# Second cross attention in units of 6, 6 and 4 heads, with expert products taken in beside it

## The reference

```python
# L1_xattn_ref: 16 heads of 16, against 77 rows of context, with masks
att = einsum('bhsd,bhtd->bhst', q, k) / sqrt(d);  att = where(mask == 0, -1e9, att)
out = einsum('bhst,bhtd->bhsd', softmax(att), v);  x = x + out
# L1_ffn_ref, attention part: 8 experts, each row weighted by a gate
n1 = layernorm(x) * w + b;  rw = gating(n1, smha_sim, smha_gates)
q, k, v = (einsum('btc,ech,bte->bth', n1, proj, rw) for proj in (q_proj, k_proj, v_proj))
attn = softmax(causal(q @ k.T * scale)) @ v
hs = x + einsum('bth,ehc,bte->btc', attn, o_proj, rw)
```

## Time and profile before

| | us |
|---|---|
| median of 3 runs | 1319.3 (1313.14 to 1320.17) |
| profiled execution, its own time | 1325.34 |
| its span | 1323.6 |
| TensorE busy in the span | 1177.9 (89%) |
| VectorE busy | 851.8 (64%) |
| ScalarE busy | 555.9 (42%) |

### The profile page before, as it was taken

The page is one execution under the profiler, slowest core; times in us unless marked ns, Lnnn a source line. Parts: engine busy times, 40 slices in busy tenths (PEclk is TensorE's granted clock), DMA queues, the critical chain, the costliest instruction groups (busy, mean ns, idle before and its releaser), DMA issues. The chain is left out here.

```text
span 1323.6 us, 19885 instructions
## 1 busy us (share of the span) xinstructions
PE 1177.9 (89%) x7124; PEld 838.7 (63%) x7124; DVE 851.8 (64%) x1832; ACT 555.9 (42%) x1209; POOL 256.6 (19%) x426
## 2 busy tenths in 40 slices
PE   8788999898888889899889788999988787899998
PEld 4343333333333348677567677999967677789888
DVE  5577777877646668556568777756534355865555
ACT  6205666665656445455235453010032333543332
POOL 5012222222220037344102220000010112400000
PEclk9979999999979779999899998999989889999999
DMA  7840373330614510000030000000030000000000
GB/s 212 202 96 2 56 64 50 50 49 25 104 22 96 103 45 18 0 0 1 0 128 1 1 1 1 1 0 1 0 128 1 1 1 0 1 0 17 17 17 16
DMA packets 38000, 50.70 MB, mean 38 GB/s; under 512 B 11130, under 2 KB 28816, under 8 KB 37264
## 3 DMA queue, kind: packets, MB, share of 16 engines
q1 hardware_dynamic: 37904, 49.44, 17.6%
HBM read 37.26 MB, written 11.77 MB: 37 GB/s over the span
## 5 line engine op out<-in xcount | busy, mean ns | idle before, releaser
L577 PE MATMUL PS<-ARENA 128*17 128x512 f32 (+19 forms) x2208 | 395.2, 426 | 62.8 <-DVE ARENA L1752 14.8
L577 PEld LDWEIGHTS PS<-ARENA 128*17 128x17 f32 (+6 forms) x2208 | 159.4, 124 | 220.3 <-issue 123.6
L1352 ACT ACTIVATE ARENA<-PS 128x512 f32<-128x512 f32 (+3 forms) x384 | 169.8, 495 | 135.7 <-PE PS L577 133.4
L1752 DVE TENSOR_REDUCE ARENA<-PS 128x1 f32<-128x128 f32 (+7 forms) x256 | 182.9, 750 | 46.1 <-PE PS L577 44.3
L577 PE MATMUL PS<-WQKVP,TRR 128*128 128x384 f32 x512 | 134.1, 344 | 1.5 <-ACT BC L1279 1.0
L2184 POOL TENSOR_SCALAR_AFFINE_SELECT ARENA<-ARENA 128x128 f32<-128x128 f32 x256 | 74.3, 299 | 224.8 <-ACT ARENA L1352 222.9
L577 PEld LDWEIGHTS PS<-W2P,INT 128*128 128x128 f32 x768 | 95.1, 188 | 2.9
L577 PE MATMUL PS<-W2P,INT 128*128 128x256 f32 x768 | 95.5, 279 | 0.0
L577 PEld LDWEIGHTS PS<-WQKVP,TRR 128*128 128x128 f32 x512 | 93.4, 192 | 2.6 <-ACT BC L1279 1.9
L2030 DVE SCALAR_TENSOR_TENSOR ARENA<-PS,rw,ARENA 128x384 f32<-128x384 f32 x112 | 69.2, 617 | 39.2 <-PE PS L577 37.9
L577 PE MATMUL PS<-TRR,W1P 128*128 128x512 f32 x256 | 88.3, 406 | 5.8 <-ACT BC L1279 5.8
(11 more groups left out here) (224 smaller groups left out, 1926.5 us busy)
## 6 DMA issues: line engine op xcount, KB each, us to landing
ARENA<-qk_parts SPq DMA_DIRECT2D x96, 128.0 KB, 5.4
ARENA<-xq_parts SPq DMA_DIRECT2D x48, 128.0 KB, 5.7
qk_parts<-ARENA SPq DMA_DIRECT2D x6, 768.0 KB, 3.3
ARENA<-in_w SPq DMA_DIRECT2D x2, 2048.0 KB, 10.5
xq_parts<-ARENA SPq DMA_DIRECT2D x8, 384.0 KB, 2.6
ARENA<-in_wqkv SPq DMA_DIRECT2D x1, 3072.0 KB, 11.4
X<-in_x SPq DMA_DIRECT2D x4, 512.0 KB, 6.7
ARENA<-in_wf SPq DMA_DIRECT2D x2, 1024.0 KB, 8.9
```

What stands on the lines that cost most here:

```text
L577: return nc.tensor.matmul(o, lhsT, rhs, start=start, stop=stop, **kw)
L1352: ins = nc.scalar.activation(PROB[GRP * (step % 2) + j][:, 0:w], PS[:, uses[key][0], 0:w], ACT.Exp, scale=HD ** -0.5)
L1752: ins = v.tensor_reduce(negm[:, n % 2, TPB * j + st:TPB * j + st + 1], PS[:, bank:bank + 2, :].rearrange("p b s -> p (b s)")[:, 0:P * (st ...
```

## The change

The cross attention is cut into three units a tile, of 6, 6 and 4 heads (462, 462 and 308 columns), 48 in all. A unit's scores now fill one bank; the units take banks 0, 1 and 2 in turn. Transposes of one unit take one bank (3 or 4 in turn), with four, four and three pieces. Values are 4, 4 and 3 fp32 matmuls of 102, 102 and 68 columns, into bank 5 for every tile. `EX` and `PTS` slots are of 512 columns, and the columns beyond the heads are cleared once by GpSimd.

One list, `expert_plan()`, now sets the order of the cross attention and of the products on TensorE, VectorE, ScalarE and GpSimd. From step 23 on it puts products beside the units, three, three and two in three steps, so that 32 products (four tiles) stand in 12 steps: those of a chunk begin in the step in which its gate is done. Until the tenth tile they take banks 6 and 7 alone, then 6, 7, 0 and 1. The normalization and gate work of a chunk is cut into halves of two tiles and spread over steps 0 to 11 behind the chunk. Products of the last eight tiles but a few stand behind the last unit. The split of the expert weights goes every second step from the eighth on (before: every third from the fourth).

In the row attention, the transposes of `P1` stand ahead of those of `ATT`. Buffers move in SBUF.

```diff
+GATE_LAG, QUOTA, WEIGHTS_AT = 23, (3, 3, 2), 8
+def chunk_ops(c, at):
+    if at == 1:
+        yield "lean", c
+    if at in (2, 3):
+        yield "stat", c, at - 2
+    if at in (4, 5):
+        yield "center", c, at - 4
+    if at in (6, 7):
+        yield "scale", c, at - 6
+    if at in (7, 8):
+        yield "turn_n1", c, at - 7
+        yield "square", c, at - 7
+    if at in (8, 9):
+        yield "lower", c, at - 8
+    if at == 9:
+        yield "logits", c
+def expert_plan():
+    period = 4 * PER_TILE
...
+        while count > 0 and sent < len(products) and u >= period * (products[sent][0] // 4) + GATE_LAG:
+            i, e = products[sent]
+            yield "product", i, e
+            if i > 0 and e == 2:
+                yield "turn_qk", i - 1
...
+    for u in range(-2, UNITS + 2 * period):
+        if u + 2 < UNITS:
+            yield "scores", u + 2
+        for at, op in ((1, "gate"), (0, "softmax")):
+            c, rest = divmod(u + at - GATE_LAG, period)
+            if rest == 0 and 0 <= c < 4:
+                yield op, c
+        if u == -1:
+            yield "context_values", 0
+        if 0 <= u + 1 < UNITS:
+            yield "probs", u + 1
+        last = u >= period * 3 + GATE_LAG
+        quota = len(products) if last else QUOTA[u % 3]
+        yield from product(1, u)
+        if 1 <= u <= UNITS:
+            yield "values", u - 1
+            if (u - 1) % PER_TILE == PER_TILE - 1:
+                yield "divide", (u - 1) // PER_TILE
+        yield from product(1, u)
+        if 0 <= u < UNITS:
+            yield "turn_probs", u
+        yield from product(quota - 2, u)
...
+        for c in range(4):
+            yield from chunk_ops(c, u - period * (c + 1))
...
-            for i in range(TILES):
-                for e in range(EXPERTS):
-                    bank = 4 + (EXPERTS * i + e) % 4
...
+                        banks = (6, 7) if n < 10 else (6, 7, 0, 1)
+                        bank = banks[products % len(banks)]
...
-                if 0 < i <= TILES:
-
-                    t = i - 1
-                    drained(pe, ("a1", t))
-                    claim(("at", t), [5, 6])
...
                 if i < TILES:
                     drained(pe, ("s1", i))
                     claim(("p1", i), [2, 3])
...
+                if 0 < i <= TILES:
+
+                    t = i - 1
+                    drained(pe, ("a1", t))
+                    claim(("at", t), [5, 6])
```

More of the change, by code:

```diff
@@ L280, in cross_plan, with unit_heads, unit_pieces, product @@
             yield (op, *at)
+GATE_LAG, QUOTA, WEIGHTS_AT = 23, (3, 3, 2), 8
+def unit_heads(u):
+    first = UH * (u % PER_TILE)
+    return first, min(HEADS, first + UH)
+def unit_pieces(u):
+    first, last = unit_heads(u)
+    return [(lo, min(P, (last - first) * T - lo)) for lo in range(0, (last - first) * T, P)]
+def chunk_ops(c, at):
[16 more added lines that the diff above has]
+    period = 4 * PER_TILE
+    products = [(i, e) for i in range(TILES) for e in range(EXPERTS)]
+    sent = 0
+    def product(count, u):
+        nonlocal sent
+        while count > 0 and sent < len(products) and u >= period * (products[sent][0] // 4) + GATE_LAG:
[3 more added lines that the diff above has]
+                yield "turn_qk", i - 1
+            sent += 1
+            count -= 1
+    for u in range(-2, UNITS + 2 * period):
[20 more added lines that the diff above has]
+        yield from product(quota - 2, u)
+        e, rest = divmod(u - WEIGHTS_AT, 2)
+        if rest == 0 and 0 <= e < EXPERTS:
+            yield "weights", e
+        for c in range(4):
+            yield from chunk_ops(c, u - period * (c + 1))
+    yield "turn_qk", TILES - 1
 def build(nc, a, out):
@@ L698, in gate_columns, with second_gate @@
+            def second_gate(u):
+                for m in range(4):
+                    c = chunk_at(u, 8 + m, 4)
+                    if c is not None:
+                        gate_turn(1, 4 * c + m, (7 if m else 4) if u < TILES + 2 else 4 - 2 * (u % 2))
+                c = chunk_at(u, 12, 4)
+                if c is not None:
+                    gate_logits(1, c, 7 if u < TILES + 2 else 5 - 2 * (u % 2))
             def gate_columns():
@@ new lines, in turn_probs, with unit_values @@
+            def turn_probs(u, bank):
+                pe.wait_ge(ex_ready, u + 1)
+                claim(("px", u), [bank])
+                for j in range(len(unit_pieces(u))):
+                    ins = nc.tensor.transpose(PS[:, bank, P * j:P * j + P], EX[u % 4][:, P * j:P * j + P], ident[:, :])
+                filled(ins, ("px", u))
+            def unit_values(u):
+                t = u // PER_TILE
+                h0, h1 = unit_heads(u)
+                if u % PER_TILE == 0:
+                    claim(("ox", t), [5])
+                if u == 0:
+                    pe.wait_ge(vx_ready, B * (len(PIECES) + 3))
+                drained(pe, ("px", u))
+                pieces = unit_pieces(u)
+                for j, (lo, rows) in enumerate(pieces):
+                    ins = mm(PS[:, 5, VW * h0:VW * h1], PTS[u % 4][0:rows, j, :],
+                             VBD[0:rows, t // TPB, u % PER_TILE, j, 0:h1 - h0, :], start=j == 0, stop=j == len(pieces) - 1)
+                if u % PER_TILE == PER_TILE - 1:
+                    filled(ins, ("ox", t))
@@ L1034, in _ @@
                     row_scores(i + 1)
+                if i < TILES:
+                    drained(pe, ("s1", i))
+                    claim(("p1", i), [2, 3])
+                    for tt in range(i % TPB + 1):
+                        ins = nc.tensor.transpose(PS[:, 2 + tt // 4, P * (tt % 4):P * (tt % 4) + P],
+                                                  P1[i % 2][:, P * tt:P * tt + P], ident[:, :])
+                    filled(ins, ("p1", i))
                 if 0 < i <= TILES:
```

558 lines of the change are left out of this document (281 added, 277 removed).

## The result

In 20 runs each, taken side by side, the kernel before takes 1319.86 us (median) and the changed one 1314.79, 5.1 us less. Some executions of any of these kernels are slower as a whole, and the ratios given here are taken without them, so they can differ a little from the ratio of the medians. The ratio is 0.9948, 95% interval 0.9924 to 0.9972: faster by 0.5%, or 6.9 us, where 13.3 were forecast. A later series gave 0.9954 (0.9924 to 0.9984). So stages are compared here by their own lengths, and whole kernels by their runs.

What follows compares the result with a forecast made beforehand. TensorE was taken as the bound where fed, VectorE binding nearly as hard in the cross attention. Cross attention and products -7.3 and row attention -6 made -13.3, from a median of 1319.3 to 1306 us; range 1289 to 1321.

Steps and rivals of the forecast that it cites:

- cross attention and products -7.3: Cross attention with products laid over its later part: 286.4 us against 293.7 before, 7.3 us less.
- row attention -6: Row attention: P1 transposes fill TensorE's waits before ATT, 5.5 us, plus half a microsecond from earlier copies; bounds 0 and -10.
- Entry: Start of the cross attention, up to the first even step: 10.3 us, against 10.0 before.
- my 2.5: Steps 24 to 47, at a gate: TensorE loses 2.5 us waiting for bank 6, behind three product readings.
- steps 12 to 23, first chunk: Cross attention, first chunk's normalization and gate work beside units: VectorE binds, 38.7 us.
- the clock, 6: Products after logits run at the lower clock level, 1.7 us lost each; three or four of four groups fall: 6 us.
- 11 steps: Cross attention steps 1 to 11, without chunk work: 22.9 us plus 0.5 for copies that no longer fit, 23.4.
- my 6.25: TensorE's time for one cross attention tile in the new units: 6.25 us against 6.02 before.
- Steps 24 to 47: Units with 64 products and gate work: 125.3 us of TensorE work, 133.5 with 4.1 lost for each of two chunks.
- the tail: Behind the last unit: 62 products, last values, gate work and transposes, with 3 us lost at the last gate: 74.5 us.
- the second rival: VectorE's list binds beside products, steps 24 to 47 losing 0.4 us more each: 1316 us; chance 0.21 with the last rival.
- The clock falls in the unit steps: Rival: shorter matmuls and more transposes drop the clock in the 23 steps without products: slower, 1330 us; chance 0.10.

Runs made afterwards that it cites:

- the first wait filled: Changed kernel with eight useless matmuls ahead of the wait at the first gate of each chunk, the wait left in place: 1309.26 us, ratio 0.9895.
- the later gate: Changed kernel with logits, gate and softmax of a chunk, and their products, one step later, logits in a transpose bank: 1302.08 us, ratio 0.9884.
- the kernel without overlap: Changed kernel with all products behind the last unit, none beside a unit: 1331.02 us, ratio 1.0116.
- bank 7: Changed kernel with logits one step later in a transpose bank, plus the second gate's first input transposes in bank 7, not 4: 1296.9 us, ratio 0.984.

## Why the prediction was right in sign and wrong in size

The time (1306 forecast, 1314.79 measured) lay in the range, and its sign was right; but the two terms were off in opposite directions. Forecast: cross attention and products -7.3, row attention -6. Measured by runs: +7 and -12.

**Entry right, idle time near by partly other waits.** 9.6 us for 10.3. Idle time in the stage fell to 17.1; I had 25 lost, 6 of them as clock, so 19. The waits at the gate were 2.15 and 2.22, where I had 1.6 and 2.5. But my 2.5 was for bank 6, behind three readings of products; the 2.22 is for bank 5, which logits and values share and which I had overlooked. That the two are so near is luck.

**The failed step: "steps 12 to 23, first chunk", 38.7, and with it the clock, 6.** It took 49.1, with TensorE busy 40.8 of it where I had 30.7 of work, and a clock of 0.83. I had priced the waits at their own length and the clock only behind the logits of the products, 1.7 each. What runs behind a gate's wait at 1.2 GHz is the whole of the logits (+2.4), the scores (+0.9), the values (+1.0) and the unit behind it. The wait of 2.43 us for ScalarE's copy, for which I had nothing, is in the 49.1 too. Over the whole stage a granted clock of 0.94 is at most 18 us lost (an estimate, 0.06 of 300.16), where I had 6. Two runs show the size: 8.4 us of the stage with the first wait filled, 14.4 with both gate waits gone. With the later gate the stage is 285.8, against the 286.4 of my sum: partly luck, since the units are dearer, as follows, and the idle time is smaller (11.2).

**The units, mis-sized.** 11 steps took 24.9 for 23.4. Values of 102 columns cost 0.11 as I took them, but I let six of 68 columns cost 0.66, and they took 0.95. The rows by shape for steps 1 to 11 (count, busy, mean ns of one):

```profile
L665 PE MATMUL PS<-ARENA 128*128 128x102 f32 x48 | 6.6, 274 | 0.0
...
L665 PE MATMUL PS<-ARENA 128*128 128x68 f32 x12 | 2.0, 288 | 0.0
...
L665 PE MATMUL PS<-ARENA 52*128 52x68 f32 x6 | 1.3, 298 | 0.0
```

One of 68 columns (288) is as long as one of 102 (274). The first tile was 0.59 us over my 6.25, the second 0.47. In the first, 0.29 of it are the six of 68 columns, 0.06 the other values, and about 0.2 scores and masks. At 0.5 us a tile this is 8 us over 16 tiles. A second estimate agrees: TensorE's busy time, less the share of the stage that the granted clock was short of 1.00, is 257 us in before's stage (268.87 - 0.04 x 293.80) and 269 with the later gate (274.54 - 0.02 x 285.78), 12 us more where I had 4. What makes the six dear lies mostly at the piece of 52 rows, as shown above; why a piece of 52 rows costs more than one of 78 or 128 was not settled.

**Steps 24 to 47 and the tail.** 138.9 and 77.3 us (step 48 begins at 876.3) for 133.5 and 74.5, with 6 for the clock apart from them: 216.2 for 214. In steps 24 to 47 TensorE was idle for 5.3 us in all, where I had 8.2: 2.8 at logits, 0.8 for bank 5, and only once for a reading of products, 1.1. Its busy time was 133.6 us for my 125.3, dearer units and the clock (0.96) together. So the second rival, waits beside the products in each step, is refuted, here and by the kernel without overlap.

**Row attention, -6, too small.** The hole filling was right in size: 5.7 of wait for my 5.5, and 13.3 in 11 places became 8.2 in 8. Missing were 2.7 of busy time, and what lies between these -9.4 (144.7 to 135.3) and the -12 of the runs. The -12 is uncertain by 4 to 6 us, so this last part may be nothing. It may also be that the old order falls to 0.90 more often, as in before's profile; a handful of profiled executions can't tell.

**The rivals.** "The clock falls in the unit steps" had the mechanism and the wrong place. Steps 1 to 11 were granted 1.00 with TensorE busy 24.89 of 24.89, 11 transposes a tile; it fell in the steps behind them, where it waits. The Trainium skill, "TensorE: Matmul & The Clock Gate", section "PE-mode transpose", says that transposes do not count as activity; at this share of them the trace shows no fall.

## What to carry to other kernels

A wait of 2 us in front of a run of thin matmuls can cost more than itself: here the next 14 us (720 to 734, a second wait among them) were granted half the clock, and VectorE, which needs their results, was idle for 7.6 us. Price a gate, and whatever else is short and late, with all that follows it until the clock is back, and try first to put it one step later. Look also for results that are read late in a bank that the next step needs: that wait of 2.2 us did not change when the logits became fast, and went with the bank. When a change has two parts, run each alone before arguing over the sum: here one gave 12 us, the other took 7, and moving one step of a list, and one bank, turned that one into a gain (stage 285.8 for 291.3 to 293.8 before the change). And fp32 matmuls of 136, 102, 68 and 8 columns with 128 columns of weights all cost 0.11 us or more here: splitting work into narrower ones saved nothing. A gain in a single pair of profiles is no gain yet: bank 7 looked like 3.6 us, and 2.6 of them were the clock.

## What was not expected of the hardware

Useless matmuls made a stage faster: eight of them in place of an idle wait, four times, took it from 300.2 us to 291.75. Yet four of them per tile in the row attention brought nothing (ratio 1.0029). And the same stretch of the same program, the row attention with the new order, was granted 0.96 in one execution (135.3 us) and 0.92 in another (140.8), with no wait moved; single profiles of this kernel can't settle 5 us there.
